# First expert layer in the order of falling tile counts, with weight splits in that order, early biases on TensorE and a double-buffered gate

## The chip, the cores and the metric

The kernel runs on one core of one Trainium2 chip. The metric is the device time in microseconds of one execution; times below are medians of several runs, and durations inside the kernel come from one profiled execution. The engines are TensorE (PE; its weight loads are listed as PEld), VectorE (DVE), ScalarE (ACT), GpSimd (POOL) and SyncE (SP), which only issues DMAs. A name with a q behind it (ACTq) is the engine's sequencer.

## The reference

A macaron block on 4 x 256 tokens of width 512: a mixture-of-experts layer, an attention layer and the same mixture-of-experts layer again, each behind a layer norm and with a residual.

```python
def ffn(x, W_gate, b_gate, W_e, b_e):          # W_e: 8 experts of 512 x 512
    logits = x @ W_gate + b_gate
    _, top_idx = jax.lax.top_k(logits, 2)
    y_all = jax.nn.relu(jnp.einsum('bsd,edh->bseh', x, W_e) + b_e)
    y = jnp.take_along_axis(y_all, top_idx[..., None], axis=2)
    return y.mean(axis=2)

x = x + 0.5 * ffn(layernorm(x), W_gate, b_gate, W_e, b_e)
x = x + attention(layernorm(x), Wqkv, bqkv, Wo, bo)   # one head of width 128, softmax over 256 keys
x = x + 0.5 * ffn(layernorm(x), W_gate, b_gate, W_e, b_e)
```

With the reference's inputs the first layer routes 248, 221, 241, 282, 295, 279, 237 and 245 (token, expert) pairs to experts 0 to 7, which is 2, 2, 2, 3, 3, 3, 2 and 2 tiles of 128 rows.

## The kernel before

The 2048 (token, expert) pairs of a mixture layer are sorted by expert and cut into tiles of 128 rows, at most NS = 23 of them; what an expert leaves empty stays empty, and tiles that no expert needs are run with no rows in them. There is no scheduler: each engine has its own program, written out by hand, and semaphores (`hi_made`, `lo_made`, `tp_copied`, `exp_done`, `ypre_made`, `yrow_made`, ...) order them against each other. An engine's instructions run in the order in which its program has them, so what stands behind a wait is late with it.

**Gate** (`gate`, `copy_gate`, `copy_logits`, `fold_logits`, `choose`). For each of four batches of two tiles TensorE transposes x, ScalarE copies the transposes to `xt_gate`, TensorE multiplies by the gate weights (less their mean, `centre_gate_weights`), ScalarE copies the result to `logit_t`, and TensorE folds four partial sums. VectorE makes the logits, the two best experts and their one-hot rows. ScalarE also writes the normalised rows (`normalise`), which SyncE stores to DRAM (`xn_dram`) for the gathers.

**Routing** (`count`, `split_rank`, `tile_starts`, `slots`, `token_list`, `tokens`, `tile_experts`). TensorE counts pairs ahead of each pair; VectorE makes from it each pair's rank, the tiles of each expert (`ntile`), the first tile of each (`excl`, a running sum) and each pair's tile and row; one-hot rows (`row_hot`) and marks go to TensorE, whose 16 small matmuls bring out the token of every row (L905). `tokens` turns that into indices (`tok`), and `tile_experts` writes the expert of every tile (`eid`). `warm_up` is matmuls of ones that keep TensorE's clock up.

**Experts** (`experts` on each engine). For tile t GpSimd gathers 128 rows of `xn_dram` (L541), TensorE transposes them (L917), ScalarE copies them, rounded, to `xt_hi` (`hi_rows`, L687) and VectorE writes what is left to `xt_lo` (`lo_rows`, L1408). The float32 product is the sum of three: hi rows by hi weights, hi rows by lo weights, lo rows by hi weights, four matmuls each (L943). VectorE adds the expert's bias from `be_bc`, a table of all biases on all partitions (`bias`, L1416), ScalarE applies relu (`relu`, L697), and GpSimd scatters the rows to `z_dram` (L549). In two cases, `t >= NY[f]`, TensorE adds the bias itself. The expert's number is read from `eid` to a register with `value_load` by TensorE and, ahead of `bias`, by VectorE.

The weights are loaded once, in 16 halves of an expert (`raw`, `load_half`), and split in the first layer: ScalarE rounds a half to `whi` (`split_hi`, L619), VectorE subtracts to `wlo` (`split_lo`, L379). Before, the halves are split in their own order: nine `hi` halves ahead of the first tile and one in each of the following, four `lo` halves ahead and two in each of tiles 0 to 5. Tile t may belong to expert t, so its product waits for the halves of experts 0 to t:

```python
if f == 0 and t < E:
    pe.wait_ge(hi_made, 2 * (t + 1))
    pe.wait_ge(lo_made, 2 * (t + 1))
```

In a tile ScalarE's program is `hi_rows(t + 1)`, `relu(t)`, split; VectorE's is `lo_rows(t + 1)`, `bias(t)`, splits.

**Second layer.** Its routing runs under the attention of the last batch. The first NA = 5 tiles are listed from the first three batches' pairs alone (`slots_early`, `token_list(1)`, `tokens(1)`), so that their gathers start before the last batch is through.

## Time and profile before

| | us |
|---|---|
| median of 3 runs | 277.38 (276.53 to 281.84) |
| the profiled execution | 278.46 |
| its span, first to last instruction | 276.6 |
| mean granted TensorE clock, share of full speed | 0.958 |
| busy: TensorE, VectorE, ScalarE, GpSimd | 243.6, 162.8, 108.2, 126.5 |

The profiled execution is 1.08 us above the median and 1.86 us longer than its span. Busy time is a sum over stages with different limits, so it doesn't say which engine a stage waits for; the chain of waits and the engines' timelines do.

### The profile page before, as it was taken

What the parts mean: (1) busy time and instruction counts of PE and PEld (TensorE: products, weight loads), DVE (VectorE), ACT (ScalarE), POOL (GpSimd) and SP (SyncE); (2) the same over time, 40 slices, a digit from 0 to 9 for tenths busy, and PEclk for the clock granted to TensorE, in tenths of its full rate; (3) what the DMA queues carried; (4) which work ended last, traced back from release to release, by engine and by line L of the source; (5) the groups of instructions that cost most, each with busy time, mean ns of one, the idle gap of its engine ahead of it and who ended that gap; (6) DMA issues with size and microseconds to landing.
All of it is one profiled execution on the core that took longest, in us unless ns stands there. A gap on an engine that the chain in (4) does not pass through costs nothing.

```text
span 276.6 us, 4889 instructions
## 1 busy us (share of the span) xinstructions
PE 243.6 (88%) x1319; PEld 181.5 (66%) x1320; DVE 162.8 (59%) x403; ACT 108.2 (39%) x192; POOL 126.5 (46%) x161
## 2 busy tenths in 40 slices
PE   6757979998999999989999995879989999999940
PEld 3543447677888888748778754347758888888730
DVE  2735679897444444766777766453963344444591
ACT  2756745454343333222336554105333433333310
POOL 5410174775665563324145510071377656664240
PEclk9995799999999999999999998699999999999995
DMA  5998889944784356154401022034246434547994
GB/s 144 396 368 309 307 253 378 359 139 150 246 262 131 124 158 186 61 154 152 152 4 46 31 78 76 0 100 150 95 152 200 164 126 135 164 126 208 334 355 172
DMA packets 22918, 49.40 MB, mean 179 GB/s; under 512 B 4460, under 2 KB 5100, under 8 KB 22640
## 3 DMA queue, kind: packets, MB, share of 16 engines
q1 hardware_dynamic: 13712, 26.55, 27.3%
q0 software_dynamic: 7360, 20.46, 23.3%
q10 hardware_dynamic: 1824, 2.12, 2.1%
q8 instruction: 11, 0.18, 0.3%
q14 instruction: 11, 0.09, 0.1%
HBM read 34.43 MB, written 18.35 MB: 191 GB/s over the span
## 4 chain that ended last, share of the span: by engine, by line
PE 67%; DVE 14%; ACT 5%; DMA 5%; issue 5%; DVEq 2%; POOL 1%; ACTq 1%; POOLq 0%
PE y_ps L943 18%; PE qk_ps L943 17%; PE tp_ps L917 6%; DVE wlo L379 5%; PE qk_ps L1018 5%; PE sp_ps L823 3%; PE tp_ps L844 3%; PE v_ps L1029 3%; DMA xg_late<-xn_dram,tok 2%; DMA bg_bc<-in_L_ffn_b_gate_dram 2%; PE y_ps L1068 2%; PE sp_ps L1056 2%; DVE ypre L1416 2%; PE g_ps L857 1%; PE sp_ps L1040 1%
## 5 line engine op out<-in xcount | busy, mean ns | idle before, releaser
L541 POOL DMA_INDIRECT xg<-xn_dram,tok x23 | 27.4, 1192 | 30.6 <-DVE tok L1330 17.9
L541 POOL DMA_INDIRECT xg_late<-xn_dram,tok x23 | 22.6, 984 | 29.5 <-DVE tok L1330 15.8
L549 POOL DMA_INDIRECT z_dram<-yrow,place x23 | 24.5, 1065 | 22.1 <-ACT yrow L697 14.4
L1408 DVE TENSOR_TENSOR xt_lo_late<-tp_ps,xt_hi_late 128x512 fp32r<-128x512 f32 x23 | 15.9, 691 | 27.9 <-ACT xt_hi_late L687 27.9
L697 ACT ACTIVATE yrow<-ypre 128x512 f32<-128x512 f32 x22 | 13.9, 633 | 44.0 <-DVE ypre L1416 44.0
L549 POOL DMA_INDIRECT z_dram<-xn,place x16 | 17.2, 1074 | 21.1 <-ACT xn L697 15.3
L1408 DVE TENSOR_TENSOR xt_lo<-tp_ps,xt_hi 128x512 fp32r<-128x512 f32 x23 | 15.9, 689 | 18.4 <-ACT xt_hi L687 18.4
L379 DVE TENSOR_TENSOR wlo<-raw,whi 128x1024 fp32r<-128x1024 f32 x16 | 18.8, 1218 | 2.6 <-POOL behind L569 2.1
L697 ACT ACTIVATE xn<-ypre_late 128x512 f32<-128x512 f32 x14 | 8.8, 632 | 26.9 <-DVE ypre_late L1416 25.8
L687 ACT ACTIVATE xt_hi_late<-tp_ps 128x512 fp32r<-128x512 f32 x23 | 13.4, 584 | 11.7 <-PE tp_ps L917 11.7
L1164 DVE BATCH_NORM_STATS2 stats<-x 128x6 f32<-128x512 f32 x24 | 15.6, 683 | 2.2 <-DMA x<-in_L_attn_x_dram 1.9
L619 ACT ACTIVATE whi<-raw 128x1024 fp32r<-128x1024 f32 x16 | 16.0, 1042 | 0.0
L1018 PE MATMUL qk_ps<-xt_att,wqkv 128*128 128x256 f32 x64 | 15.6, 390 | 0.4 <-ACT xt_att L671 0.4
L917 PE MATMUL tp_ps<-ident,xg_late 128*128 128x128 f32 x92 | 13.8, 274 | 2.2 <-DMA xg_late<-xn_dram,tok 2.2
L943 PE MATMUL y_ps<-whi,xt_hi 128*128 x48 | 14.5, 423 | 1.3 <-DVE wlo L379 1.3
L823 PE MATMUL sp_ps<-ones 128*128 128x512 bf16 x50 | 15.1, 462 | 0.0
L917 PEld LDWEIGHTS tp_ps<-ident,xg_late 128*128 128x128 f32 x92 | 11.1, 141 | 5.9 <-DMA xg_late<-xn_dram,tok 3.1
L917 PE MATMUL tp_ps<-ident,xg 128*128 128x128 f32 x92 | 13.9, 273 | 1.1 <-DMA xg<-xn_dram,tok 1.1
L943 PE MATMUL y_ps<-whi,xt_hi_late 128*128 x48 | 14.4, 421 | 0.5 <-ACT xt_hi_late L687 0.5
L687 ACT ACTIVATE xt_hi<-tp_ps 128x512 fp32r<-128x512 f32 x23 | 13.4, 582 | 3.5 <-PE tp_ps L917 3.5
L529 POOL TENSOR_TENSOR rstd<-var_eps,neg_half 128x2 f32<-128x2 f32 x12 | 8.9, 740 | 12.7 <-DVE var_eps L1179 12.1
L917 PEld LDWEIGHTS tp_ps<-ident,xg 128*128 128x128 f32 x92 | 11.3, 140 | 4.8 <-DMA xg<-xn_dram,tok 2.0
(197 smaller groups left out, 547.4 us busy)
## 6 DMA issues: line engine op xcount, KB each, us to landing
raw<-in_L_ffn_W_e_dram SPq DMA_DIRECT2D x16, 512.0 KB, 8.5
z_rows<-z_dram SPq DMA_DIRECT2D x6, 512.0 KB, 3.7
x<-in_L_attn_x_dram SPq DMA_DIRECT2D x8, 256.0 KB, 6.6
be_bc<-in_L_ffn_b_e_dram SPq DMA_DIRECT2D x2, 1024.0 KB, 9.5
xn_dram<-xn ACTq DMA_DIRECT2D x8, 256.0 KB, 2.0
whi<-z_dram SPq DMA_DIRECT2D x4, 512.0 KB, 5.3
wlo<-z_dram SPq DMA_DIRECT2D x4, 512.0 KB, 6.6
out_dram<-x SPq DMA_DIRECT2D x8, 256.0 KB, 3.0
```

The costliest lines, as they stand in the source:

```text
L379: eng.tensor_tensor(half(wlo, n), half(raw, n), half(whi, n).bitcast(F32), ALU.subtract).then_inc(done, 1)
L541: pool.indirect_dma_start(out=xg_at(f, t % XG), out_offset=None, in_=xn_dram[f][0:T - S if f and t < NA else T, :], in_offset=bass.Indirec ...
L549: pool.indirect_dma_start(out=z_dram[f][:, :], out_offset=bass.IndirectOffsetOnAxis(ap=place[:, t:t + 1], axis=0), in_=yrow_at(f, t % YB), ...
L619: act.activation(half(whi, n), half(raw, n), ACT.Copy).then_inc(hi_made, 1)
L687: act.activation(xt_hi_at(f, t % 2), tp_ps[(n0 + t) % 2][:], ACT.Copy).then_inc(tp_copied, 1)
L697: act.activation(yrow_at(f, t % YB), ypre_at(f, t % 2) if t < NY[f] else y_ps[t % 2][:], ACT.Relu, scale=HALF_MEAN).then_inc(yrow_made, 1)
L823: pe.matmul(bank[:], ones[:], ones[:].unsqueeze(1).broadcast_to([P, 4, P]), start=True, stop=True)
L917: last = pe.transpose(tp_ps[(n0 + t) % 2][:, c * P:(c + 1) * P], xg_at(f, t % XG)[:, c * P:(c + 1) * P], ident[:])
L943: last = pe.matmul(y_ps[t % 2][:], rows[:, c * P:(c + 1) * P], w[:, bass.ds(e * WE + c * H, H)], start=(n == 0), stop=(rows is lo and c == ...
L1018: last = pe.matmul(qk_ps[:, j * S:(j + 1) * S], wqkv[:, c, j * D:(j + 1) * D], xt_att[:, c, :], start=(c == 0), stop=(c == NC - 1))
L1164: read.append(step(dve.bn_stats(stats[:, s + i, :], x[:, TB * b + i, :])))
L1408: dve.tensor_tensor(xt_lo_at(f, t % 2), tp_ps[(n0 + t) % 2][:], xt_hi_at(f, t % 2).bitcast(F32), ALU.subtract).then_inc(xt_made, 1)
```

## The change

- **Order.** `tile_starts(0)` no longer takes a running sum over the experts. It makes a key of each expert from its tile count and its number, compares all pairs of keys (`bigger`), and sums the tile counts of the experts ahead (`excl`): experts come by falling count, ties by number. `order_experts` writes the expert at each place to `turn`, and twice that plus two, the number of halves that must have landed. `tile_experts_ordered` makes `eid` from both ends of each expert's stretch. `places` goes by `start_t`, so that the pairs' two halves of `z_dram` follow the new order; it moves from ahead of `tile_starts` to inside `slots`.
- **Splits.** `split_hi` and `split_lo` take the expert from `turn` by `value_load`. `split_hi` waits for one semaphore, `landed_halves`, which SyncE raises in the order of the halves. By the falling order the first 2E tiles need one new expert for two tiles; product t waits for `2 * (t // 2 + 1)` halves. Ahead of the first tile four `hi` and two `lo` halves are split; then `HI_IN_TILE` and `LO_IN_TILE`. VectorE's and ScalarE's heads of straight code are ten tiles (`HEADS`) and no longer eight.
- **Biases.** In tiles 0 to 3 of layer one TensorE adds the bias, from rows in three bf16 parts (`be_rows`, made by ScalarE and GpSimd) picked by `sel`; relu then reads the product itself. The tables `be_bc` are loaded after all halves, since their space serves the gate's second buffer, the gate weights' staging and `be_raw` until then.
- **Gate.** `xt_gate_at` and `gate_ps_at` alternate between two buffers and two banks in layer one, and the programs of TensorE and ScalarE are written out in a new order. Three tiles of x come by ScalarE's queue and the gate bias by SyncE's. The filling matmuls stand between the counts, 4, 5 and 6, and 18 ahead of the list, in place of 6 and 14.
- **Second layer.** ScalarE's copy for the gate goes ahead of a normalised tile and of two stores; the counts go ahead of projection matmuls; `slots_early` takes `score_max` into its middle; `token_list(1)` runs ahead of `mix_v`, ScalarE's mark ahead of `copy_prob`; filling matmuls, 3 and 7, stand around the scores. The third row buffer of the layer is a slot of `xn` (`yrow_at`).

```diff
+    BIAS_PE = (list(range(4)) + [NS - 1], [NS - 2, NS - 1])
+    BIAS_FROM = min(t for t in range(NS) if t not in BIAS_PE[0])
...
-        HI_AHEAD = 9
-        LO_AHEAD = 4
-        LO_IN_TILE = [2, 2, 2, 2, 2, 2]
+        HI_AHEAD = 4
+        LO_AHEAD = 2
+        HI_IN_TILE = [2, 2, 2, 2, 1, 1, 1, 1]
+        LO_IN_TILE = [2, 2, 2, 2, 1, 1, 1, 1, 1, 1]
+        X_BY_SP = 5
...
+            for i in range(X_BY_SP):
                 sp.dma_start(x[:, i, :], x_rows[i * P:(i + 1) * P, :]).then_inc(x_in_sem[i], 16)
+            sp.dma_start(bg_bc[:], b_gate.partition_broadcast(P)).then_inc(gate_bias_in, 16)
             for n in range(LOAD_FIRST):
                 load_half(n)
+            sp.wait_ge(be_zeroed, 1)
+            for first in (0, BE_LO, 2 * BE_LO):
+                sp.dma_start(be_raw[first:first + E, :], b_e).then_inc(be_rows_in, 16)
             for i in range(NT):
                 sp.wait_ge(xg_made, i + 1)
                 sp.dma_start(xn_dram[0][i * P:(i + 1) * P, :], xn_at(i)).then_inc(xn_stored[i], 16)
-            load_be(0)
+            def report_landed(first, end):
+                for n in range(first, end):
+                    sp.wait_ge(raw_in[n], 16)
+                    sp.sem_inc(landed_halves, 1)
             for n in range(LOAD_FIRST, LOAD_AHEAD):
                 load_half(n)
+            report_landed(0, LOAD_AHEAD)
...
+            sp.wait_ge(gate_done, B)
+            sp.wait_ge(be_rows_made, 2)
+            load_be(0)
             load_be(1)
+            report_landed(LOAD_AHEAD, 2 * E)
...
             def split_hi(n):
-                act.wait_ge(raw_in[n], 16)
-                act.activation(half(whi, n), half(raw, n), ACT.Copy).then_inc(hi_made, 1)
+                if n == 0:
+                    act.wait_ge(turn_made, 1)
+                e = act.value_load(turn[0:1, 0, n // 2:n // 2 + 1], min_val=0, max_val=E - 1)
+                if n % 2 == 0:
+                    loaded = act.value_load(turn[0:1, 1, n // 2:n // 2 + 1], min_val=2, max_val=2 * E)
+                    act.wait_ge(landed_halves, loaded)
+                act.activation(half_of(whi, e, n), half_of(raw, e, n), ACT.Copy).then_inc(hi_made, 1)
...
                 for t in range(head + first * STEP):
                     tile(t)
-                    if hi_left:
-                        split_hi(hi_left.pop(0))
+                    if f == 0 and t < len(HI_IN_TILE):
+                        for _ in range(HI_IN_TILE[t]):
+                            split_hi(hi_left.pop(0))
...
-                        pe.wait_ge(ypre_made, read)
-                    if f == 0 and t < E:
-                        pe.wait_ge(hi_made, 2 * (t + 1))
-                        pe.wait_ge(lo_made, 2 * (t + 1))
+                        pe.wait_ge(yrow_made if t - 2 in BIAS_PE[f] else ypre_made, read)
+                    if f == 0 and t < 2 * E:
+                        pe.wait_ge(hi_made, 2 * (t // 2 + 1))
                     n = 0
-                    if t >= NY[f]:
-                        pe.matmul(y_ps[t % 2][:], ident[:], be_bc[:, bass.ds(e * H, H)], start=True, stop=False)
+                    if t in BIAS_PE[f]:
+                        if f == 0 and t < BIAS_FROM:
+                            pe.matmul(y_ps[t % 2][:], sel[:, bass.ds(e, 1)].broadcast_to([BE_ROWS, P]),
+                                      be_rows[:], start=True, stop=False)
+                        else:
+                            pe.matmul(y_ps[t % 2][:], ident[:], be_bc[:, bass.ds(e * H, H)], start=True, stop=False)
...
+                        if w is wlo:
+                            if f == 0 and t < 2 * E:
+                                pe.wait_ge(lo_made, 2 * (t // 2 + 1))
...
+            copy_gate(0, 0)
+            copy_gate(0, 1)
+            copy_logits(0, 0)
+            normalise_batch(0, 0)
+            copy_gate(0, 2)
+            copy_logits(0, 1)
+            normalise_batch(0, 1)
+            copy_gate(0, 3)
+            copy_logits(0, 2)
+            copy_logits(0, 3)
+            normalise_batch(0, 2)
+            normalise_batch(0, 3)
+            bias_rows_high()
             mark_partition(0)
-            for n in his:
+            for n in range(HI_AHEAD):
...
+            count(0, 0)
+            warm_up(4, sp_ps)
+            count(0, 1)
+            warm_up(5, sp_ps)
+            count(0, 2)
             warm_up(6, sp_ps)
-            for b in range(B):
-                count(0, b)
-            warm_up(14, sp_ps)
+            count(0, 3)
+            warm_up(18, sp_ps)
             token_list(0)
...
+            count(1, b - 1)
+            warm_up(3, y0_ps)
             scores(b)
-            count(1, b - 1)
+            warm_up(7, y0_ps)
             transpose_prob(b)
+            token_list(1)
             mix_v(b)
-            project_out(b, lambda: token_list(1))
+            project_out(b)
...
+            def order_experts():
+                link(dve.tensor_reduce(position, bigger[0:1], AX_X, ALU.add))
+                link(dve.tensor_tensor(at_turn, position.unsqueeze(1).broadcast_to([1, E, E]),
+                                       iota_e[0:1, :].unsqueeze(2).broadcast_to([1, E, E]), ALU.is_equal))
+                link(dve.tensor_tensor(at_turn, at_turn, iota_e[0:1, :].unsqueeze(1).broadcast_to([1, E, E]),
+                                       ALU.mult))
+                link(dve.tensor_reduce(turn_f, at_turn, AX_X, ALU.add))
+                step(dve.tensor_copy(turn[:, 0, :], turn_f))
+                link(dve.tensor_scalar(turn[:, 1, :], turn_f, 2.0, 2.0, ALU.mult, ALU.add))
+                dve.engine_nop().then_inc(turn_made, 1)
...
+                    tile_step = step(dve.scalar_tensor_tensor(out=key[:], in0=ntile[:], scalar=float(E),
+                                                              in1=from_last[:], op0=ALU.mult, op1=ALU.add))
+                    dve.wait_ge(dve_step, rank_step)
+                    rank_row(B - n, n).then_inc(row_made, n)
+                    dve.wait_ge(dve_step, tile_step)
+                    tile_step = step(dve.tensor_tensor(bigger, key[:].unsqueeze(1).broadcast_to([P, E, E]),
+                                                       key[:].unsqueeze(2).broadcast_to([P, E, E]), ALU.is_gt))
+                    step(rank_tile(B - n, n))
+                    dve.wait_ge(dve_step, tile_step)
+                    link(dve.tensor_tensor(ahead_of, bigger, ntile[:].unsqueeze(1).broadcast_to([P, E, E]),
+                                           ALU.mult))
+                    link(dve.tensor_reduce(excl[:], ahead_of, AX_X, ALU.add))
...
+            def split_lo(n):
+                e = dve.value_load(turn[0:1, 0, n // 2:n // 2 + 1], min_val=0, max_val=E - 1)
+                dve.wait_ge(hi_made, n + 1)
+                dve.tensor_tensor(half_of(wlo, e, n), half_of(raw, e, n), half_of(whi, e, n).bitcast(F32),
+                                  ALU.subtract).then_inc(lo_made, 1)
...
-            places(0, B)
             tile_starts(0)
             slots(0)
+            order_experts()
             tokens(0)
-            tile_experts(0)
+            tile_experts_ordered()
             dve.wait_ge(first_issued, 1)
             for n in range(LO_AHEAD):
-                split_lo(dve, n, lo_made)
+                split_lo(n)
...
-            slots_early()
+            slots_early(lambda: score_max(b))
```

The new order of instructions at three places. First ScalarE, from its mark of the partitions to its second tile of layer one. Before:

```order
L677 ACTIVATE mark<-in_tile,part_id 128x368
L619 ACTIVATE whi<-raw 128x1024 x6
L687 ACTIVATE xt_hi<-tp_ps 128x512
L619 ACTIVATE whi<-raw 128x1024
L687 ACTIVATE xt_hi<-tp_ps 128x512
L697 ACTIVATE yrow<-ypre 128x512
L619 ACTIVATE whi<-raw 128x1024
L687 ACTIVATE xt_hi<-tp_ps 128x512
L697 ACTIVATE yrow<-ypre 128x512
L619 ACTIVATE whi<-raw 128x1024
```

After, from the first copy of rows on (the four splits that stand ahead of it read in the same way; L672 and L674 read the expert and the landed count, L676 is the split):

```order
L753 ACTIVATE xt_hi<-tp_ps 128x512 x2
L765 ACTIVATE yrow<-y_ps 128x512
L672 TENSOR_LOAD turn
L672 ISA x2
L674 TENSOR_LOAD turn
L674 ISA x2
L676 ISA
L676 ACTIVATE whi<-raw 128x1024
L672 TENSOR_LOAD turn
L672 ISA x2
L676 ISA
L676 ACTIVATE whi<-raw 128x1024
```

Every split has one or two register reads ahead of it, two splits stand in a tile where one stood, and the relu of tile 0 reads the product itself. Second, VectorE between the second set of one-hot rows and its first splits. Before:

```order
L1281 TENSOR_TENSOR row_hot<-iota_r,slot_r 128x1024
L1327 TENSOR_SCALAR place_lo<-g_ps 128x23
L1329 TENSOR_TENSOR place<-g_ps,place_lo 128x23
L1330 TENSOR_SCALAR tok<-place 128x23
L1289 TENSOR_TENSOR passed<-iota_t,incl 1x184
L1291 TENSOR_REDUCE eid_f<-passed 1x23
L1292 TENSOR_SCALAR eid<-eid_f 1x23
L379 TENSOR_TENSOR wlo<-raw,whi 128x1024 x4
```

After (`used` and `picked` serve `order_experts` as scratch):

```order
L1378 TENSOR_TENSOR row_hot<-iota_r,slot_r 128x1024
L1386 TENSOR_REDUCE used<-above 1x8
L1387 TENSOR_TENSOR picked<-used,iota_e 1x64
L1389 TENSOR_TENSOR picked<-picked,iota_e 1x64
L1391 TENSOR_REDUCE used<-picked 1x8
L1392 CAST turn<-used 1x8
L1393 TENSOR_SCALAR turn<-used 1x8
L1394 ISA
L1452 TENSOR_SCALAR place_lo<-g_ps 128x23
L1454 TENSOR_TENSOR place<-g_ps,place_lo 128x23
L1455 TENSOR_SCALAR tok<-place 128x23
```

The order of the experts (L1386 to L1393) stands ahead of the token arithmetic. Third, TensorE from the last projection of attention to the second layer's first transposes. Before:

```order
L1018 MATMUL qk_ps<-xt_att,wqkv 128x256 x2
L1040 MATMUL sp_ps<-qk 128x256 x2
...
L1048 MATMUL sp_ps<-ident,prob 128x128 x4
L1056 MATMUL sp_ps<-pt,v 128x256 x2
L1068 MATMUL y_ps<-wo,prob 128x512
L905 MATMUL v_ps<-mark_a,row_hot 128x10 x12
L1068 MATMUL qk_ps<-wo,prob 128x512
L823 MATMUL sp_ps<-ones 128x512 x11
L917 MATMUL tp_ps<-ident,xg_late 128x128 x4
```

After:

```order
L1100 MATMUL qk_ps<-xt_att,wqkv 128x256 x2
...
L893 MATMUL y_ps<-ones 128x512 x3
L1122 MATMUL sp_ps<-qk 128x256 x2
L893 MATMUL y_ps<-ones 128x512 x7
L1130 MATMUL sp_ps<-ident,prob 128x128 x4
L974 MATMUL v_ps<-mark_a,row_hot 128x10 x12
L1138 MATMUL sp_ps<-pt,v 128x256 x2
L1150 MATMUL y_ps<-wo,prob 128x512
L1150 MATMUL qk_ps<-wo,prob 128x512
L893 MATMUL sp_ps<-ones 128x512 x11
L986 MATMUL tp_ps<-ident,xg_late 128x128 x4
```

The list (`v_ps<-mark_a,row_hot`) moved from between the output matmuls to behind the transposes of `prob`, and ten filling matmuls are new.

## Rows read from the trace of the kernel before

**Rows 1.** The page: engines' busy time; a costly group (count | busy us, mean ns | idle).
```profile
PE 243.6 (88%) x1319; PEld 181.5 (66%) x1320; DVE 162.8 (59%) x403; ACT 108.2 (39%) x192; POOL 126.5 (46%) x161
...
L379 DVE TENSOR_TENSOR wlo<-raw,whi 128x1024 fp32r<-128x1024 f32 x16 | 18.8, 1218 | 2.6 <-POOL behind L569 2.1
```

**Rows 2.** Chain of waits in order of time: start us, us, what.
```profile
7.37 1.07 PE v_ps L864 x8
...
25.82 5.81 PE sp_ps L823 x14
...
179.92 3.47 DMA xg_late<-xn_dram,tok
```

**Rows 3.** Timelines of ScalarE and TensorE, end of the gate: start us, us, instruction.
```profile
16.82 1.09 ACT L654 ACTIVATE xt_gate<-tp_ps 128x512 f32<-128x512 f32 x2 [1.98 <-PE tp_ps L844]
...
19.83 2.92 ACT L632 ACTIVATE xn_more<-x,off,rstd 128x512 f32<-128x512 f32 x4
...
19.98 0.61 PE L871 MATMUL g_ps<-fold,logit_t 128*128 128x8 f32 x4 [0.50 <-ACT logit_t L663]
```

**Rows 4.** Timeline of VectorE, routing of layer one.
```profile
23.27 0.22 DVE L1248 TENSOR_TENSOR picked<-onehot,rk_ps 128x64 f32<-128x64 bf16 x1 [3.18 <-PE rk_ps L894]
...
25.30 1.22 DVE L1281 TENSOR_TENSOR row_hot<-iota_r,slot_r 128x1024 bf16<-128x1024 bf16 x1
...
26.81 0.21 DVE L1248 TENSOR_TENSOR picked<-onehot,rk_ps 128x64 f32<-128x64 bf16 x1
...
29.88 1.22 DVE L1281 TENSOR_TENSOR row_hot<-iota_r,slot_r 128x1024 bf16<-128x1024 bf16 x1
```

**Rows 5.** Timeline of TensorE: token list, first product, products of tiles 9 and 10.
```profile
31.46 0.57 PE L905 MATMUL g_ps<-mark,row_hot 128*128 128x46 bf16 x16
...
38.19 1.19 PE L943 MATMUL y_ps<-whi,xt_hi 128*128 x4 [0.32 <-DVE wlo L379]
...
71.95 1.17 PE L943 MATMUL qk_ps<-whi,xt_hi 128*128 x4
...
75.18 1.17 PE L943 MATMUL y_ps<-whi,xt_hi 128*128 x4
```

**Rows 6.** Timeline of GpSimd: the first gather.
```profile
32.98 1.22 POOL L541 DMA_INDIRECT xg<-xn_dram,tok  x1 [17.85 <-DVE tok L1330]
```

**Rows 7.** Timelines of VectorE and ScalarE around tile 4.
```profile
57.17 0.69 DVE L1408 TENSOR_TENSOR xt_lo<-tp_ps,xt_hi 128x512 fp32r<-128x512 f32 x1
...
58.02 0.69 DVE L1416 TENSOR_TENSOR ypre<-y_ps,be_bc 128x512 f32<-128x512 f32 x1 [0.15 <-issue]
...
58.74 0.63 ACT L697 ACTIVATE yrow<-ypre 128x512 f32<-128x512 f32 x1 [1.67 <-DVE ypre L1416]
59.28 1.04 ACT L619 ACTIVATE whi<-raw 128x1024 fp32r<-128x1024 f32 x1
60.23 0.58 ACT L687 ACTIVATE xt_hi<-tp_ps 128x512 fp32r<-128x512 f32 x1
```

**Rows 8.** VectorE's sequencer in the bias (L1412), all of it: ns min/median/max.
```profile
L1412 DVEq TENSOR_LOAD <-eid x43: 299/306/1142, 41.5 to 257.1; - x43
```

**Rows 9.** Stretches: length, busy PE, PEld, DVE, ACT, POOL, clock share, DMA, GB/s.
```profile
21.10:24.50 3.40, 2.43 (x28) 1.40 (x26) 1.06 (x8) 3.40 (x5) 0.00 (x0) 0.50 0.80 294
...
171.30:174.70 3.40, 2.17 (x7) 1.59 (x8) 3.16 (x19) 1.09 (x4) 0.00 (x0) 0.50 0.00 0
```

**Rows 10.** Timeline of VectorE and TensorE ahead of the second layer.
```profile
169.84 0.69 DVE L1523 TENSOR_REDUCE soft<-sp_ps 128x2 f32<-128x512 f32 x1 [1.60 <-PE sp_ps L1040]
...
173.64 2.07 PE L1056 MATMUL sp_ps<-pt,v 128*128 128x256 f32 x4 [0.69 <-ACT pt L756]
...
174.54 0.68 DVE L1281 TENSOR_TENSOR row_hot<-iota_r,slot_r 128x512 bf16<-128x512 bf16 x1
...
178.05 0.47 PE L905 MATMUL v_ps<-mark_a,row_hot 128*128 128x10 bf16 x12
...
184.92 1.21 PE L943 MATMUL y_ps<-whi,xt_hi_late 128*128 x4 [0.19 <-ACT xt_hi_late L687]
```

269 lines of the change are left out of this document (179 added, 90 removed).

## The prediction

> **What bounds the kernel now.** I read the page first: TensorE is busy for 88% of the span [rows 1], so I asked where it runs at its own pace and where it waits. The chain of waits answers in order of time. From tile 8 of the first expert layer on, TensorE is never late: one tile's matmuls follow the last one's after 3.23 us (71.95, 75.18) [rows 5]. There less work would help, and the change takes none away. Three stretches are not TensorE's. (a) **Before the first product**, at 38.19 us: the gate, which starts late because the gate weights' sum waits for the gate bias (7.37 us) and then goes back and forth between TensorE and ScalarE, 3.34 us a batch; then routing on VectorE, with 14 filling matmuls of TensorE as the last step ahead of the token list at 31.46 [rows 2, 5]. (b) **Tiles 0 to 8 of layer one**: tile 0 starts at 38.19 us and tile 9 at 71.95 us, 33.8 us for nine tiles that TensorE could do in nine times 3.23, 29.0. Two things set it, each 3.7 us long: VectorE's two splits of 1.22 us with bias and low rows of 0.69 each [rows 1, 7]; and a cycle from VectorE's bias (58.02) over ScalarE's relu (58.74), its half of a weight (59.28) and its copy of rows (60.23) to the next low rows and bias [rows 7]. (c) **Ahead of the second layer**: TensorE waits for scores, softmax and the first gather, and its clock is at half after 171 us [rows 9, 10].
>
> **Routing, the gate.** Two buffers and two banks let a batch's transposes run under the last one's gate. ScalarE becomes the limit: two copies (1.0 from start to start), logits 0.3, two normalised tiles 1.4 [rows 3], 2.7 us a batch. From about 9.6 us (a second batch of x that can't be used earlier) twice 2.7, then 1.3, then gate, copy and fold of the last batch, 1.6: the last fold ends at about 17.9, where it ended at 20.59 [rows 3].
>
> **Routing, VectorE.** Count, four filling matmuls and count end near 19.4. Then ranks and choose (2.0 from 23.27 to 25.30) and one-hot rows (1.2) [rows 4] bring the second rank pick to 22.7; before, it was 26.81. From there to the last one-hot rows before took 26.81 to 31.10, 4.3 us. Added on that path: comparing 64 keys, a product and a reduction of 64 in place of two steps of 8 (0.6 us by their neighbours of 0.2), and the places, moved here behind the slots (0.4). 22.7 + 5.3 makes 28.1 for 31.10. Next stands the ordering of the experts, seven linked steps, 1.5 us, ahead of the token arithmetic: TensorE's list (0.57) is hidden under it. Tokens end at 30.3, before at 32.68; GpSimd's gather starts 0.3 later and its rows are there 3.5 us after its start, at about 34.1 [rows 5, 6].
>
> **Routing, what is late next.** The table of tile experts grows to three steps over 368 elements, some 2.8 us against 0.9, and ends at 33.1, before the rows land: hidden. ScalarE is late next. Its first split now waits for the order, at 29.6, and it does four in a row ahead of the first copy of rows. Each reads the expert's number into a register. ScalarE never does so in this trace. The nearest row is VectorE's read: a TENSOR_LOAD of 306 ns in the median, once 1142 [rows 8], and register work behind it: the bias starts 0.85 us after the low rows ahead of it (57.17, 58.02), which keep the engine for 0.69 [rows 7]. The lower bound is nothing (it runs ahead under an activation of 1.04 us), the upper is that 1.14. I take 0.55, since an engine that has just passed its semaphore starts the read only then: before the bias, the read starts with the operation ahead of it. An even half reads twice (number and landed count): 1.3 us. So the splits start at 31.0, 32.0, 33.3 and 34.2, the copy at 35.2, and the first product at 35.9 for 38.19: **2.3 us earlier**. Loading x by two queues, and the bias rows that GpSimd and ScalarE make (some 5 us of GpSimd's, idle from 15 to 33), I cost at nothing: they lie beside that work, and if they ended after 30 us the gather would wait for them.
>
> **Tiles 0 to 8.** The order of falling counts asks two halves for two tiles, not for one. The reference's counts make it 3, 4, 5, 0, 1, 2, 6, 7, so the third expert's halves are numbers 10 and 11, whose loads start after the first gather, as before. They are needed on ScalarE near 40.8; with their issue 2.4 us earlier they should be there by 40.4. VectorE gets lighter: two splits and the low rows, 3.1 us, with no bias in tiles 0 to 3. TensorE pays one more matmul of 0.23 us for four tiles. ScalarE gets heavier: relu, two reads (1.3), split, read (hidden), split, copy of rows. From the end of product t to the start of product t + 2 it needs 3.9 us, which TensorE's 3.5 a tile doesn't cover: about 3.7 us a tile, as before. From tile 4 on the bias is on VectorE again and the cycle closes: copy 0.6, bias 0.8 after it and 0.7 long, relu, read of 1.3 or 0.7, split. By the durations of [rows 7] the starts of products follow each other by 4.4, 3.8, 4.4 and 3.8 us, where before they took 3.7. Added up, tile 9 starts 34.9 us after tile 0, against 33.8: **1.1 us lost**, although half as many splits are asked. If the reads hid wholly, 9 times 3.23 and 4 times 0.23 would be 30.0. Both bias tables load now after the halves; by their rate they are there at about 54.5, when VectorE comes for them; up to 1.5 us late is in the range.
>
> **Ahead of the second layer.** Three moves. The gate copy no longer stands behind ScalarE's issue of two stores, and the count goes ahead of two projection matmuls: scores are there 0.7 us earlier than at 169.84. The slots' first steps run while VectorE would wait for scores, 1.6 us of idle [rows 10]. The list of tokens runs ahead of the mixing of V, when the last one-hot rows are made: these end at 172.7 for 175.22. The list before ran at 178.05, between the output matmuls. Tokens then end at 173.8, and the first gather goes out at 174.6 for 179.92 and lands at 178.1 for 183.4 [rows 2, 10]. What is late next: the output projection and its residual, which the table of experts stands behind. Ten more filling matmuls cover the waits, and I take the clock to stay at full. Then four transposes end at 171.7, the list at 173.2, V's mix takes 1.0 for 2.07, the projection likewise half of before and ends at 176.3, the table is there at 179.1, warm-up ends at 178.7, and transposes and copy bring the first product to 180.1 for 184.92: **4.9 us earlier**. All behind it hangs on that product.
>
> **Sum.** 2.3 - 1.1 + 4.9 = 6.1 us. The profiled execution took 278.46 us (span 276.6 and 1.9 around it), 1.1 above the median; 272.4 for it is 271.3 on the median of 277.38.
>
> **Rivals.** *The reads hide.* If ScalarE's sequencer reads while it waits, stretch (b) takes 30.0 us: 4.9 less, 266.4. Against it speaks where VectorE's reads stand in the trace: none starts before the wait ahead of it ends.
> *The filling stays at half clock.* The clock was at half from 21.1 us and still in the 14 filling matmuls, 0.42 us each [rows 2, 9], after a gate in which TensorE stood between its matmuls. The change makes the gate denser and puts 33 filling matmuls in for 20. If the clock falls all the same, 18 of them at 0.43 us hold the list to 33.6 where it stood at 31.46, and the first gain turns from 2.3 to a loss of 2.1: 275.7.
> *The second transition keeps its half clock.* Transposes, mix (2.07) [rows 10] and projection stay as long as they were; the earlier list alone leaves the first product at 182.2: 273.5.
> *Slower than before: dear reads.* The cost is ScalarE's, from turn_made to tile 7. With loads of twice the median, four that count ahead of the first copy add 1.5 us, three in each of tiles 0 to 3 add 3.6, and six in tiles 4 to 7 add 1.8: 6.9 us, 278.2. It passes the time before from a load of 0.57 us on. For it speaks VectorE's longest load, 1.14 [rows 8]; against it their median.
> The Trainium skill (DMA: Bandwidth & Descriptors, Latency and other measured facts) gives a tensor_load a floor of some 600 ns. By that rule this rival is the forecast; the trace's median of 306 ns disagrees.
>
> **How the numbers follow.** Forecast 271.3, chance 0.45, its own range 269.3 to 273.3 (0.7 each way for x's arrival, 1.5 for late bias tables). Hidden reads 0.13; half clock in the first filling 0.14; in the second 0.14; dear reads 0.07; the rest, 0.07, is mixtures. The range 267.5 to 276 takes the forecast, both clock cases and part of the first, some 0.8. A change of 2%, to 271.8, is about what a measurement of this kernel can tell from none. Faster by over 2%: 0.28 of the forecast's 0.45, hidden reads at 0.13 and 0.05 of mixtures, 0.46. Slower by over 2%, above 282.9, needs loads over 0.8 us: 0.03. Within 2%: 0.51.
>
> **What the profile would show.** Last fold at about 18; full clock from 14 to 30 us; first product near 36; TENSOR_LOAD rows on ScalarE near 0.3 us and idle time of some 0.7 us ahead of the first split of a tile; tile 9 starting near 70.8; full clock from 168 to 180 and the gain growing by 4 to 5 us up to the first late product. I am wrong if tiles 4 to 7 run at 3.2 us, if the clock row shows 0.5 in either filling, or if splits wait for landed_halves or VectorE for the bias tables.

## The result

The changed kernel takes **282.3 us** (281.55 to 285.81, 4 runs) where the kernel before takes 276.97 (276.53 to 281.84, 4 runs): ratio 1.0183, 95% interval 1.0145 to 1.0221. It is slower, by 5.3 us; whether by more than 2% the interval leaves open. The forecast was 271.3, its range 267.5 to 276.0. The profiled execution took 281.96 us, span 279.7, mean granted clock 0.964; a second trace of the same program, taken later, 283.52 and 281.3. Disturbed runs are left out of the comparisons.

The page of the changed kernel has the same engine times as before, within 5 us [rows 1], so the loss has to be looked for stage by stage, in waits and in work at half clock.

```profile
PE 247.4 (88%) x1346; PEld 184.0 (66%) x1347; DVE 165.7 (59%) x413; ACT 109.1 (39%) x194; POOL 130.7 (47%) x173
```

TensorE's timeline (... stands for rows left out), which answers to [rows 5] and the last row of [rows 10] (list, first product, tiles 1, 2, 5 to 10, first late product):

```profile
30.93 0.37 PE L974 MATMUL g_ps<-mark,row_hot 128*128 128x46 bf16 x8 [0.70 <-DVE row_hot L1378]
...
39.21 2.06 PE L1018 MATMUL y_ps<-whi,xt_hi 128*128 x4
...
43.53 1.25 PE L1018 MATMUL qk_ps<-whi,xt_hi 128*128 x4
...
49.17 0.39 PE L1001 MATMUL y_ps<-be_rows,sel 72*128 72x512 bf16 x1 [2.09 <-ACT xt_hi L753]
...
60.32 0.97 PE L1018 MATMUL qk_ps<-whi,xt_hi 128*128 x3 [0.17 <-ACT xt_hi L753]
...
64.76 1.19 PE L1018 MATMUL y_ps<-whi,xt_hi 128*128 x4 [0.94 <-ACT xt_hi L753]
...
68.66 1.19 PE L1018 MATMUL qk_ps<-whi,xt_hi 128*128 x4 [0.41 <-ACT xt_hi L753]
...
72.98 1.19 PE L1018 MATMUL y_ps<-whi,xt_hi 128*128 x4 [0.83 <-ACT xt_hi L753]
...
76.88 1.20 PE L1018 MATMUL qk_ps<-whi,xt_hi 128*128 x4 [0.40 <-ACT xt_hi L753]
...
80.13 1.17 PE L1018 MATMUL y_ps<-whi,xt_hi 128*128 x4
...
185.04 1.22 PE L1018 MATMUL y_ps<-whi,xt_hi_late 128*128 x4 [0.24 <-ACT xt_hi_late L753]
```

The first product comes at 39.21 for 38.19, tile 10 at 80.13 for 75.18, the first late product at 185.04 for 184.92. So 1.0 us is lost up to the first product, 3.9 from there to tile 10, and 4.8 is gained in the second transition. Two more losses stand behind it: 0.6 in the second layer, and 2.4 at the end, where GpSimd's last scatter took 3.81 us. 1.0 + 3.9 - 4.8 + 0.6 + 2.4 is the 3.1 between the two spans (279.7, 276.6). The rest of the 5.3 between the medians: the profiled execution before lies 1.5 us above its median, the changed one 0.3 below, and the changed kernel takes 0.4 us more outside its span.

VectorE in the routing, which answers to [rows 4] (ranks, cast, rows; the same again; order of the experts; tokens), and GpSimd beside it:

```profile
20.79 0.22 DVE L1345 TENSOR_TENSOR picked<-onehot,rk_ps 128x64 f32<-128x64 bf16 x1 [2.77 <-PE rk_ps L963]
...
21.30 0.72 DVE L1355 CAST rank_u<-rank_f 128x8 uint32<-128x8 f32 x1
22.12 0.57 DVE L1359 TENSOR_SCALAR slot_r<-rank_u 128x8 uint32<-128x8 uint32 x1
...
23.54 1.06 DVE L1321 TENSOR_TENSOR onehot<-iota_e,topi 128x32 bf16<-128x32 f32 x1
...
25.66 0.21 DVE L1345 TENSOR_TENSOR picked<-onehot,rk_ps 128x64 f32<-128x64 bf16 x1
...
29.66 1.22 DVE L1378 TENSOR_TENSOR row_hot<-iota_r,slot_r 128x1024 bf16<-128x1024 bf16 x1
...
31.84 0.15 DVE L1393 TENSOR_SCALAR turn<-used 1x8 int32<-1x8 f32 x1
...
32.46 0.18 DVE L1455 TENSOR_SCALAR tok<-place 128x23 uint32<-128x23 uint32 x1
...
20.84 1.15 POOL L635 TENSOR_TENSOR be_bc<-be_bc,be_rows 72x512 f32<-72x512 f32 x1 [6.50 <-ACT be_rows L683]
22.06 0.60 POOL L636 CAST be_rows<-be_bc 32x512 bf16<-32x512 f32 x1
...
23.40 1.15 POOL L638 TENSOR_TENSOR be_rows<-be_bc,be_rows 8x512 bf16<-8x512 f32 x1
...
33.52 1.22 POOL L568 DMA_INDIRECT xg<-xn_dram,tok  x1 [8.97 <-DVE tok L1455]
```

Three of VectorE's small steps (21.30, 22.12 and 23.54) take 0.4 to 0.9 us more than the same steps before, which took 0.17, 0.17 and 0.19, and each ends when a step of GpSimd on the bias rows ends: 22.02 beside 21.99, 22.69 beside 22.66, 24.60 beside 24.55.

Two waits between 39 and 50 us (engine, line, what for: us, times, longest), the splits that the first of them held, and TensorE's clock in two stretches (length, busy times, clock share, DMA share, GB/s):

```profile
ACT whi L676 <- SPq L435: 2.4, 1, 2.4
PE y_ps L1001 <- ACT xt_hi L753: 2.1, 1, 2.1
```

```profile
46.55 2.00 ACT L676 ACTIVATE whi<-raw  x2 [2.36 <-SPq L435]
```

```profile
16.00:24.00 8.00, 7.47 (x53) 3.96 (x46) 4.03 (x23) 3.81 (x7) 2.95 (x4) 0.57 1.05 381
...
36.00:42.00 6.00, 4.81 (x16) 3.29 (x17) 2.99 (x3) 2.02 (x3) 1.98 (x3) 0.72 0.73 191
```

L435 is the report of landed halves. After the relu of tile 0 ScalarE reads its registers until 44.64 us and then stands until 46.44 for halves 10 and 11, which the third expert in line needs; its copy of rows for tile 2 stands behind these splits. With GpSimd's hold on VectorE and these halves, the half clock is the third loss: the first product's four matmuls take 2.06 us for 1.19 in [rows 5].

From tile 0 to tile 10, of the 3.9 us lost 0.6 is in tile 0 (half clock), 1.9 in tile 1 (the wait for the halves) and 1.4 in tiles 2 to 9, where ScalarE's register reads are (reads_ahead, below).

### The profile page after: what moved, and what is told of

It is laid out like the page before. It is cut to its first block, busy times and chain, and to the rows that moved or that the text cites. A ratio compares the mean times of both kernels' runs of the same rounds, so it can differ in the third digit from the quotient of the medians.

```text
span 279.7 us, 5124 instructions
## 1 busy us (share of the span) xinstructions
PE 247.4 (88%) x1346; PEld 184.0 (66%) x1347; DVE 165.7 (59%) x413; ACT 109.1 (39%) x194; POOL 130.7 (47%) x173
## 4 chain that ended last, share of the span: by engine, by line
PE 64%; DVE 9%; DMA 7%; ACT 6%; issue 6%; POOLq 1%; ACTq 1%; POOL 1%; SPq 1%; DVEq 1%
PE y_ps L1018 17%; PE qk_ps L1018 17%; PE tp_ps L986 5%; PE qk_ps L1100 5%; DMA raw<-in_L_ffn_W_e_dram 5%; PE tp_ps L914 3%; PE v_ps L1111 3%; PE rk_ps L893 2%; PE y_ps L1150 2%; PE sp_ps L893 1%; POOLq L51 1%; PE sp_ps L1138 1%; DMA xg<-xn_dram,tok 1%; DMA xg_late<-xn_dram,tok 1%; DVE row_hot L1378 1%
## 5 line engine op out<-in xcount | busy, mean ns | idle before, releaser
L576 POOL DMA_INDIRECT z_dram<-xn,place x23 | 26.6, 1158 | 26.9 <-ACT xn L765 17.8
L576 POOL DMA_INDIRECT z_dram<-yrow,place x23 | 25.3, 1101 | 25.3 <-ACT yrow L765 19.5
L568 POOL DMA_INDIRECT xg<-xn_dram,tok x23 | 23.6, 1028 | 25.9 <-PE tp_ps L986 12.8
L765 ACT ACTIVATE xn<-ypre_late 128x512 f32<-128x512 f32 x21 | 13.3, 632 | 41.6 <-DVE ypre_late L1564 41.2
L765 ACT ACTIVATE yrow<-ypre 128x512 f32<-128x512 f32 x18 | 11.4, 632 | 35.2 <-DVE ypre L1564 35.2
L1547 DVE TENSOR_TENSOR wlo<-raw,whi x16 | 19.2, 1224 | 4.9 <-ACT whi L676 2.3
L676 ACT ACTIVATE whi<-raw x16 | 16.2, 1052 | 8.5 <-issue 5.5
L893 PE MATMUL sp_ps<-ones 128*128 128x512 bf16 x63 | 17.1, 423 | 0.0
L1018 PE MATMUL y_ps<-whi,xt_hi 128*128 x48 | 15.4, 444 | 1.8 <-ACT xt_hi L753 1.8
L556 POOL TENSOR_TENSOR rstd<-var_eps,neg_half 128x2 f32<-128x2 f32 x12 | 8.9, 740 | 12.8 <-DVE var_eps L1275 12.1
```

Of the source, the lines that this page charges most:

```text
L568: pool.indirect_dma_start(out=xg_at(f, t % XG), out_offset=None, in_=xn_dram[f][0:T - S if f and t < NA else T, :], in_offset=bass.Indirec ...
L576: pool.indirect_dma_start(out=z_dram[f][:, :], out_offset=bass.IndirectOffsetOnAxis(ap=place[:, t:t + 1], axis=0), in_=yrow_at(f, t % YB), ...
L676: act.activation(half_of(whi, e, n), half_of(raw, e, n), ACT.Copy).then_inc(hi_made, 1)
L765: act.activation(yrow_at(f, t % YB), y_ps[t % 2][:] if t in BIAS_PE[f] else ypre_at(f, t % 2), ACT.Relu, scale=HALF_MEAN).then_inc(yrow_ma ...
L893: pe.matmul(bank[:], ones[:], ones[:].unsqueeze(1).broadcast_to([P, 4, P]), start=True, stop=True)
L1018: last = pe.matmul(y_ps[t % 2][:], rows[:, c * P:(c + 1) * P], w[:, bass.ds(e * WE + c * H, H)], start=(n == 0), stop=(rows is lo and c == ...
```

## The experiments

Thirteen kernels ran, two of them with a second trace. The table has each trace's stages in us: VectorE's first pick of ranks, tokens ready, start of tiles 0, 1, 2 and 10, first late product, TensorE's last end, length of the last scatter, span; and the median of its runs. A ratio behind a time is to the kernel before, run beside it: its medians were 277.7, 277.7 and 277.4, and 280.6 beside third_gather.

| kernel | ranks | tokens | tile 0 | tile 1 | tile 2 | tile 10 | late | PE end | scatter | span | median |
|---|---|---|---|---|---|---|---|---|---|---|---|
| before | 23.3 | 32.7 | 38.2 | 41.9 | 45.7 | 75.2 | 184.9 | 266.0 | 1.40 | 276.6 | 277.0 |
| before_again | 25.5 | 34.4 | 39.9 | 43.6 | 47.5 | 76.9 | 185.7 | 267.6 | 2.60 | 279.5 | one run |
| changed | 20.8 | 32.6 | 39.2 | 43.5 | 49.3 | 80.1 | 185.0 | 266.7 | 3.81 | 279.7 | 282.3 |
| after_again | 21.7 | 33.8 | 39.9 | 43.4 | 50.9 | 84.4 | 189.3 | 270.7 | 1.41 | 281.3 | 282.4 |
| low_early | 18.7 | 29.2 | 35.3 | 38.8 | 46.1 | 78.4 | 183.3 | 264.9 | 1.40 | 275.6 | 278.3 |
| halves_early | 18.6 | 30.7 | 36.8 | 40.3 | 44.3 | 76.3 | 181.2 | 262.6 | 1.40 | 273.5 | 277.0 |
| reads_ahead | 21.6 | 33.7 | 39.7 | 43.3 | 50.4 | 81.0 | 186.0 | 267.5 | 1.41 | 278.1 | 279.7 |
| scatter_gap | 20.8 | 32.6 | 39.1 | 43.5 | 49.1 | 80.0 | 185.0 | 266.5 | 0.98 | 276.8 | 280.1 |
| gate_filled | 19.5 | 31.6 | 37.6 | 41.1 | 48.4 | 79.3 | 184.2 | 265.7 | 1.40 | 277.2 | 280.8 |
| third_gather | 21.7 | 33.7 | 39.9 | 43.3 | 52.4 | 83.7 | 188.7 | 270.0 | 1.40 | 280.7 | 281.8 |
| four | 21.7 | 32.2 | 38.2 | 41.7 | 45.7 | 75.1 | 180.0 | 261.7 | 0.98 | 272.0 | 274.7 |
| four_fill | 22.1 | 32.3 | 38.4 | 42.0 | 45.9 | 75.2 | 180.1 | 261.3 | 0.98 | 271.6 | 273.7 |
| late_only | 23.6 | 32.5 | 38.0 | 41.7 | 45.6 | 75.2 | 180.0 | 262.6 | 1.40 | 273.2 | 275.7 |
| gate_late | 18.8 | 27.9 | 34.8 | 38.9 | 43.2 | 72.5 | 177.3 | 261.4 | 1.40 | 272.1 | 273.3 |
| gate_late_fill | 21.7 | 30.7 | 36.9 | 40.2 | 44.4 | 73.9 | 178.8 | 260.2 | 0.98 | 270.5 | 270.5 |

The column of first ranks moves by 3.1 us between programs whose gate is the same (18.6 in halves_early, 21.7 in after_again), and by 2.2 between two traces of the kernel before. So stages are compared from row to row of one trace, not by their absolute times.

### low_early: GpSimd's bias rows out of VectorE's way

```diff
-            for n in range(LOAD_FIRST):
+            for n in range(3):
...
             copy_logits(0, 2)
+            bias_rows_high()
             copy_logits(0, 3)
             normalise_batch(0, 2)
             normalise_batch(0, 3)
-            bias_rows_high()
```

> The changed kernel, with the bias rows of layer one made earlier: ScalarE rounds them ahead of its copy of the fourth batch's logits, so that GpSimd's four steps on them end before VectorE picks the first ranks. Theory (shared port): in the changed kernel VectorE's cast (0.72 us for 0.17), its next step (0.57 for 0.17) and its one-hot step (1.06 for 0.19) each ended when a GpSimd step on the bias rows ended; 1.8 us of the routing is this. They go back to 0.17 to 0.19 here, the second pick of ranks comes at 23.9 for 25.66, the first product at 37.4 for 39.21, and the time falls by 1.8 us to 280.5. Rival (not the port): the long steps belong to this point of VectorE's program or to the half clock around it; they stay long, GpSimd or not, and the time stays at 282.3.

Measured 278.28 us, 1.0048 of the kernel before (0.9999 to 1.0097). VectorE in it:

```profile
19.21 0.42 DVE L1357 CAST rank_u<-rank_f 128x8 uint32<-128x8 f32 x1
19.73 0.17 DVE L1361 TENSOR_SCALAR slot_r<-rank_u 128x8 uint32<-128x8 uint32 x1
...
20.97 0.19 DVE L1323 TENSOR_TENSOR onehot<-iota_e,topi 128x32 bf16<-128x32 f32 x1
...
18.44 1.15 POOL L640 TENSOR_TENSOR be_rows<-be_bc,be_rows 8x512 bf16<-8x512 f32 x1
```

The long steps are gone, but for one, and that ends with GpSimd's last (19.63 beside 19.59). From the first ranks to the tokens it takes 10.5 us; in the seven traces that have the bias rows late, 11.8 to 12.1. So GpSimd's steps beside VectorE's cost 1.3 to 1.6 us, shown, whichever of VectorE's steps is hit. The gain of 4.0 us over the changed kernel, where 1.8 was expected, is not all this edit's: the first ranks themselves are 2.1 us earlier, as they are in halves_early without it. And of the first product's 3.9 us only 1.8 is left at tile 10, because tile 2 waits for the halves all the longer (46.1 - 38.8 = 7.3 us for tile 1).

### halves_early: the late halves

```diff
-        LOAD_AHEAD = 10
-        LOAD_BETWEEN = 12
+        LOAD_AHEAD = 12
+        LOAD_BETWEEN = 14
```

> The changed kernel, with halves 10 and 11 loaded straight behind halves 6 to 9 and not behind the first gather (12 and 13 behind the first, 14 and 15 behind the second). Theory: tile 0's split waits for landed_halves from 44.64 to 46.44 us because these two halves are asked for only after the first gather has landed; without it the third product starts 1.8 us earlier and the time falls to 280.5. Rival (the next one is late too): the four halves behind them or the gather, which then shares the queues with more weights, take the wait's place; the gain is under 0.5 us, 281.8 or more.

Measured 276.97 us, 0.997 of the kernel before (0.9917 to 1.0023): level with it. Tile 1 takes 4.0 us, where it takes 5.7 to 7.5 in the six traces with the loads as the change has them. The rival fell: ScalarE's wait for the report is 0.5 us. From tile 0 to tile 10 it takes 39.5 us, the changed kernel 40.9 and 44.5 in its two traces, the kernel before 37.0; so the wait is shown, and the reads' share stays. More than the expected 1.8 came back: 5.3 us between the medians. The wait is longer in the second trace of the changed kernel (below), and this trace has early first ranks and a short last scatter; how the 5.3 divides is not shown.

### reads_ahead: the register reads

```diff
                     if t + 1 < NS:
                         hi_rows(t + 1, n0 + t + 2, f * NS + t or None)
+                    if f == 0 and t < len(HI_IN_TILE):
+                        for n in hi_left[:HI_IN_TILE[t]]:
+                            turn_read.append(read_turn(n))
...
                     relu(t, ypre_no(f, t) + 1, sent(t) or None)
```

> The changed kernel, with ScalarE's register reads for a tile's splits put ahead of the relu of that tile and not behind it. Theory (reads on the cycle): tiles 4 to 7 follow each other by 4.44, 3.90, 4.32 and 3.90 us because a split comes 0.55 or 1.3 us after the relu; with the reads done under the wait for the product they fall to the 3.7 us that VectorE's bias and ScalarE's copy set before, 1.8 us less, 280.5. Rival (reads are hidden anyway, VectorE's splits set the pace): the starts of the products stay as far apart as they are, 282.3.

Measured 279.69 us, 1.0077 (1.0039 to 1.0114). Four successive tiles:

```profile
63.35 1.17 PE L1029 MATMUL qk_ps<-whi,xt_hi 128*128 x4
...
66.84 1.25 PE L1029 MATMUL y_ps<-whi,xt_hi 128*128 x4
...
70.49 1.19 PE L1029 MATMUL qk_ps<-whi,xt_hi 128*128 x4
...
74.14 1.19 PE L1029 MATMUL y_ps<-whi,xt_hi 128*128 x4 [0.16 <-ACT xt_hi L760]
...
77.79 1.19 PE L1029 MATMUL qk_ps<-whi,xt_hi 128*128 x4 [0.16 <-ACT xt_hi L760]
```

Tiles 5 to 9 follow each other by 3.49, 3.65, 3.65 and 3.65 us, for 4.44, 3.90, 4.32 and 3.90: 2.1 us, where the theory had 1.8. The reads were on the cycle, and placed under the wait for the product they cost nothing that shows here.

### scatter_gap: the last scatter

```diff
             for i in range(NT):
+                if i == 3:
+                    dve.wait_ge(last_issued, 1)
                 dve.wait_ge(lower_added, i // 2 + 1)
```

> The changed kernel, with VectorE waiting, ahead of the fourth of its last eight additions, until GpSimd has issued the last scatter. Theory (VectorE's additions hold the scatter): the last scatter took GpSimd 3.81 us, from 268.10 to 0.86 us after VectorE's last addition, where the kernel before had gaps between the additions and took 1.40; with the gap it takes about 1.4, the end of GpSimd's program, 7.6 us after it, comes 2.3 us earlier, and the time falls to 280.0. Rival (the scatter is slow by itself, by its rows or its queue): it still takes 3.8 us, VectorE only loses the wait, and the time is 282.3 to 283.

Measured 280.12 us, 1.0110 (1.0055 to 1.0166). GpSimd's last scatter in the changed kernel and VectorE's additions beside it:

```profile
268.10 3.81 POOL L576 DMA_INDIRECT z_dram<-xn,place  x1 [2.15 <-ACT xn L765]
...
266.15 2.49 DVE L1735 TENSOR_TENSOR x<-x,whi 128x512 f32<-128x512 f32 x4
268.56 2.49 DVE L1735 TENSOR_TENSOR x<-x,wlo 128x512 f32<-128x512 f32 x4
```

With the pause:

```profile
267.89 0.98 POOL L578 DMA_INDIRECT z_dram<-xn,place  x1 [2.16 <-ACT xn L769]
...
268.98 0.69 DVE L1741 TENSOR_TENSOR x<-x,whi 128x512 f32<-128x512 f32 x1 [1.17 <-POOL behind_last L616]
```

The scatter takes 0.98 in all four kernels that have the pause. Without it, it takes 1.40 in nine of eleven traces, 2.60 in one and 3.81 in one, and the additions stand at the same places beside it in most of them: each of these scatters ends 0.86 us behind the end of an addition. For 3.81 it is the last of the eight (271.05), for 2.60 the sixth, for 1.40 the fourth, the first that ends after the scatter began. So VectorE's additions do hold the scatter, and which of their ends lets it in is chance, different from one execution to the next. It is a loss of 2.4 us in the profiled run, not one of the change. That the median fell by 2.2 us as well, as expected, is not explained by it: the second trace of the changed kernel has 1.41, where the pause could save 0.4.

### gate_filled: the clock in the gate

```diff
             transpose_xn("g0", 2, 1, 2)
+            warm_up(2)
             transpose_xn("g0", 3, 0, 1)
             gate(0, 2)
             fold_logits(0, 1)
+            warm_up(2)
             transpose_xn("g0", 3, 1, 2)
+            warm_up(3)
             gate(0, 3)
+            warm_up(2)
```

> The changed kernel with nine more filling matmuls (2, 2, 3 and 2) in TensorE's gaps between the transposes of the third and fourth batch and the gates, where it waits 0.5 to 0.8 us for ScalarE. Theory (the clock falls because TensorE stands in the gate): the granted clock stays full from 14 to 24 us, the first ranks are picked near 19.0 for 20.79, and the mean clock of a run rises from 0.965 to 0.98; 280.5. Rival (where the clock falls doesn't hang on these gaps but on where a run stands when it starts): clock and time are as they were, or 0.5 us longer for the matmuls, 282.3 to 282.8.

Measured 280.79 us, 1.0153 (1.0104 to 1.0202), clocks 0.971 to 0.978 for 0.961 to 0.969. The gate ran at full clock here, but it did so too in after_again without these matmuls. In both traces the clock fell behind a gap of 2.3 us ahead of the list instead (26.4 to 28.8 us here, half from 29.5 to 32.9). So it is inconclusive on the gate.

### four and four_fill: the mends together

four has the four edits above except the fillings. four_fill adds those, 24 filling matmuls ahead of the list for 18 and 26 behind it for 16.

> The changed kernel with the four edits tried so far together: bias rows early, halves 10 and 11 early, reads ahead of the relu, and VectorE's pause for the last scatter. Theory: they touch four different stretches, so the gains add: 1.3 (port) + 1.8 (landed halves) + 1.8 (reads) + 2.3 (last scatter) = 7.2, 275.1. Rival (the stretches depend on each other: an earlier first product meets the next late transfer, and the clock falls elsewhere): half of it, 278.5.

> The changed kernel with the four edits, the nine filling matmuls in the gate, 24 ahead of the list for 18 and 26 behind it for 16. Theory (the clock falls where TensorE stands, at the gate's end, ahead of the list and ahead of the first gather's landing): full clock from the gate to tile 9 in every run, mean clock 0.985 or more, and the time of the best run of the four edits (271.1) becomes the median. Rival (the clock's fall hangs on where an execution starts, not on these gaps; more fillings only hold the list up): 274.7 as before, or up to 1 us more.

four: 274.67 us, 0.9862 (0.9735 to 0.9989); 7.6 us under the changed kernel, 7.2 expected. Its runs lie from 271.12 to 275.35. That the two agree is luck: measured one by one, the edits' medians lay 4.0, 5.3, 2.6 and 2.2 us under the changed kernel's, 14.1 together, and half of that came of all four. So the gains don't add, as the rival said. four_fill: 273.67 us, 0.9846 (0.9789 to 0.9902), clocks 0.985 or 0.986 in every run. Its clock in the stretches where the changed kernel had 0.57 and 0.72:

```profile
16.00:24.00 8.00, 7.37 (x69) 4.36 (x69) 3.79 (x31) 5.81 (x11) 3.50 (x4) 1.00 0.89 329
...
36.00:42.00 6.00, 5.67 (x29) 3.50 (x27) 3.27 (x4) 2.30 (x4) 2.84 (x3) 1.00 0.71 194
```

Full clock in this trace and a mean of 0.985 in every run, as expected; the median did not reach the 271.1 of four's best run, and the 1.0 us to four's median is within the noise of either.

### late_only, gate_late, gate_late_fill: the parts without the order

The kernel before with the second layer's hunks of the change; with those of the first gate as well; and with more fillings and the pause, by which the third differs from the second:

```diff
-        WARM = [16, 0, 0]
+        WARM = [26, 0, 0]
...
-            warm_up(18, sp_ps)
+            warm_up(24, sp_ps)
```

> The kernel before with the second layer's parts of the change alone: the gate copy ahead of the stores, the counts ahead of projection matmuls, 3 and 7 filling matmuls around the scores, the maximum of the scores inside the early slots, the mark and the token list ahead of the mixing of V. Expert order, splits, biases and the first gate are as before. Theory: this part is worth what the prediction gave it, 4.9 us from the last product of layer one to the first late product (69.6 us before, 64.6 in the changed kernel), and nothing of it is given back: 272.5 on a median of 277.4. Rival (it shows only behind the changed layer one, or its half clock comes back without it): under 2.5 us, 275 or more.

> The kernel before with the second layer's parts and the first gate of the change: two buffers and two banks, x by two queues, the gate bias by the other queue, 4, 5, 6 and 18 filling matmuls. Expert order, splits and biases are as before. Theory: without the ordering (about 1.1 us between the first and the second rows) and without GpSimd's bias rows (1.3 to 1.8 us), the gate's gain comes through: first ranks at 20.8 at the latest for 23.27, first product near 35.5 for 38.19, 270 in all. Rival (the weights are late next: nine high and four low halves ahead of the first product, which have to land first): the first product stays near 38 and the time is that of the second layer's parts alone, 272.5.

> The kernel before with the second layer's parts and the first gate of the change, 24 filling matmuls ahead of the list for 18, 26 behind it for 16, and VectorE's pause for the last scatter. In the trace without these the clock was at half from 32.5 to 37 us, after TensorE had stood 2.24 us ahead of the first gather's rows; the first product's four matmuls took 1.98 us for 1.19. Theory: the clock stays full there, the first tile is 1.2 us shorter, and the last scatter, at 1.40, gets 0.4 shorter: 271.8 for 273.3. Rival: the fillings hold the list or the transposes up by as much, 273.3 to 274.3.

late_only: 275.7 us over ten scattered runs, 0.9904 (0.9851 to 0.9958), 272.5 expected. From tile 10 to the first late product it takes 104.8 us for 109.7, the whole 4.9, but the rows of the second layer's tile 5 then took 5.4 us from issue to landing (3.3 in the kernel before) and 1.5 us was lost again behind it. gate_late: 273.34 us, 0.987 (0.9815 to 0.9924), 270 expected: the first product at 34.8, though its four matmuls ran at half clock, 1.98 us; 3.0 us were lost again from the second layer's tile 5 on, whose rows took 5.5 us to land and behind which the clock was at half for 3.4 us. gate_late_fill: **270.54 us, 0.9743 (0.9694 to 0.9792)**, 271.8 expected, the best of all; its clock row is at 9 throughout, and TensorE has no gap ahead of the gather's rows. Its profiled execution, 272.2 us, is the slowest of its four:

```profile
PEclk9999999999999999999999999999999999999995
```

```profile
29.90 5.77 PE L846 MATMUL sp_ps<-ones 128*128 128x512 bf16 x26
35.51 0.60 PE L940 MATMUL tp_ps<-ident,xg 128*128 128x128 f32 x4
...
36.88 1.20 PE L966 MATMUL y_ps<-whi,xt_hi 128*128 x4
```

### after_again and before_again: what one trace is worth

> The changed kernel once more, unedited, for a second trace. Theory (its four losses are the program's own): clock at half in the gate's end and again at the first product, first ranks picked at 20.8, second at 25.7, 1.8 us of waiting for landed_halves in tile 0, the last scatter at 3.8 us; 282.3. Rival (part of them is the hazard of one execution): the port and the landed halves show again, but the clock falls elsewhere or the last scatter takes 1.4 us, and the time is nearer 280.

> The kernel before once more, unedited, for a second trace. Theory: the same stages within 0.5 us, the clock at half somewhere between 20 and 32 us, first product at 38.2, first late product 184.9 less what the first stage gains, 276.5 to 278. Rival: where the clock falls moves a stage by over 1 us.

after_again: 282.39 us, 1.0155 (1.0089 to 1.0222). The losses by GpSimd's bias rows (12.1 us from ranks to tokens) and of the halves are there again, the latter far larger: tile 1 takes 7.5 us, ScalarE waits 3.6 us for the report where it waited 1.8, and the clock is at half from 49 to 56 us behind it. The chain of waits shows whose wait it is:

```profile
34.70 3.59 DMA xg<-xn_dram,tok
...
38.73 9.29 DMA raw<-in_L_ffn_W_e_dram
```

The gate kept its full clock and the last scatter took 1.41, so those two were chance in the profiled run. The rival was right in this, but the time did not come nearer to 280. before_again, one run, took 281.22 us where 276.5 to 278 was expected; its first ranks are 2.2 us later than in the first trace, and 1.5 of this is there at 12 us, long before its clock fell. So a stage did move by over 1 us, as the rival said, but mostly not by the clock.

### third_gather: why the halves take so long

The first load asked for behind the first gather's landing takes 3.6 to 4.6 us to land in the five traces with splits in their own order, and 6.9 to 7.5 in the nine with ordered splits. In the five, VectorE's splits hold the third gather's issue (1.84 to 1.87 us; 0.95 in the nine). In four of them it so ends about 1.1 us behind the start of the load's issue (37.63 and 36.54 us in the kernel before). gate_late is the exception: there the gather's issue ended at 32.80, just ahead of the load's at 32.89, and the load still landed in 3.6 us. First the kernel before, then gate_late:

```profile
35.76 1.87 POOL L541 DMA_INDIRECT xg<-xn_dram,tok  x1 [0.21 <-issue]
```

```profile
30.96 1.84 POOL L552 DMA_INDIRECT xg<-xn_dram,tok  x1 [0.24 <-issue]
```

```diff
             for n in range(LOAD_AHEAD, LOAD_BETWEEN):
                 load_half(n)
+            sp.sem_inc(halves_asked, 1)
...
+                    if f == 0 and t == 2:
+                        pool.wait_ge(halves_asked, 1)
                     gather(f, t)
```

> The changed kernel, with GpSimd issuing the third gather only once SyncE has issued the loads of halves 10 and 11. In the seven traces of kernels with ordered splits the first load behind the first gather's landing took 6.9 to 7.5 us from issue to landing, in the five with splits in their own order 3.6 to 4.6; in those five VectorE's splits held the third gather's issue (1.85 us for 0.94), so that it ended behind the load's issue. Theory (the third gather's rows are fetched ahead of the weights when it is issued first, and cost them 3 us): with the gather behind, halves 10 and 11 land in 3.6 to 5 and 5 to 6.5 us, near 41.5 and 43.3 where the first product is at 39.2, the wait for landed_halves goes, and the time falls by 2 to 4 us to 278.3 to 280.3. Rival (the load's time is set by something else in the ordered kernels): 7 us again, the wait stays, and the time is 282.3 or, by the later third gather, a little more.

From issue to landing, least, median and most, of the six loads behind the first gather; first the kernel before (issued from 36.5 us), then the changed kernel (from 37.2), then this one (from 38.3). The least is the first load:

```profile
DMA to landing us min/median/max: 4.6/8.4/10.5
```

```profile
DMA to landing us min/median/max: 7.1/10.1/13.2
```

```profile
DMA to landing us min/median/max: 4.9/7.8/12.1
```

The first load lands in 4.9 us and ScalarE's wait for the report falls to 0.7, so in this kernel the gather ahead did cost the load 2 to 3 us, by one trace against nine. By gate_late, the order of the two issues is not all that sets it. And the third gather, now behind the loads, itself took 10.1 us, and tile 2 started later still (52.4). The median is 281.82 us, 1.0142 (1.0007 to 1.0276) of a kernel before whose runs beside it ranged from 275.7 to 282.3: no gain. Changing the order of the two moved the wait from the halves to the gather; what took it away in these runs was asking for the halves earlier.

## Why the prediction was wrong, point by point

The forecast was 6.1 us faster, and the profiled execution's span is 3.1 longer. Of these 9.2 us, 3.3 lie ahead of the first product (35.9 forecast, 39.2 measured) and 2.8 from there to tile 9 (34.9 forecast, 37.7 measured); 0.1 is the second transition, 0.6 lies in the second layer behind it and 2.4 in the last scatter, of which the sum had nothing.

**The second transition** was right, term and mechanism: 4.8 us for 4.9, full clock, first gather out at 179.30 in a layer that ran 5 us late; late_only shows it alone, though its median is only 2 us under the kernel before's.

**The reads and the cycle** were right. A split's read begins when the wait ahead of it ends (TENSOR_LOAD some 277 ns, the longest 500), and tiles 5 to 8 took 4.44, 3.90, 4.32 and 3.90 where the text had 4.4, 3.8, 4.4, 3.8, one tile sooner. That ScalarE takes the reads behind the relu was worth 2.1 us, which the sum had inside its 1.1. VectorE did not wait for the bias tables.

**The step that failed first** was "with their issue 2.4 us earlier they should be there by 40.4". The halves 10 and 11 landed at 44.3 and 46.4 us, and in the second trace at 45.8 and 48.0. Their issue was 0.6 us later than before, not earlier, since the gather was (33.52 for 32.98), and they took 7.1 and 8.8 us to land for 4.6 and 5.8. I had read the time to landing in the trace of the kernel before as a property of the load. third_gather shows that in this kernel it hangs on the gather ahead of it, which VectorE's splits no longer held; why gate_late's load was fast all the same stays open. The wait, 1.8 us in the profiled run and 3.6 in the second, where half clock follows it, is the loss whose mending gained most: halves_early takes it away and is level with the kernel before.

**The second failure** was "I cost at nothing: they lie beside that work". GpSimd's steps on the bias rows, 20.84 to 24.55 us, fell on VectorE's ranks and held three of its steps, 1.3 to 1.6 us: the second pick of ranks came 4.9 us behind the first, where the forecast had 3.3. I looked at GpSimd's idle time and not at what it shares. The Trainium skill (SBUF — State Buffer, Who interferes with whom) has VectorE and GpSimd share a pair of ports under an exclusive lock. By it a VectorE cast or tensor_scalar can take the pair, an operation with two inputs in SBUF contends with a GpSimd instruction that reads SBUF, and a reduction never contends. The trace agrees: the cast, the tensor_scalar and the one-hot step held here are of these kinds (0.72 us for 0.17, 0.57 for 0.17, 1.06 for 0.19), and the reduction and the maxima beside GpSimd's steps kept their length (0.22 and 0.16). The page spoke against the change, and I did not weigh it.

**The filling stays at half clock** was a rival at 0.14, and in the profiled run the clock did fall: 0.57 of full clock from 16 to 24 us, the first four fillings in 1.89 us, and again at the first product. In other traces the fall came elsewhere. What the rival priced did not happen: the eighteen fillings ahead of the list ran at full clock, in 4.04 us, and the list was not late by them. The first ranks came 1.4 us late (20.8 for 19.4), of which the fall explains 1.3 (last folds 1.02 us for 0.61, first fillings 1.89 for 1.02 in halves_early); ahead of the first product it cost some 1.0 more (transposes 0.88 us for 0.60, three fillings 1.49 for 0.81). With the 1.6 of the second failure, less 0.6 that the steps from the second ranks to the tokens were shorter than forecast, this is the 3.3 us of the first product: the tokens were ready at 32.6 for 30.3, and the first split could start only at 33.52 for 31.0. Without the order the first product is at 34.8 (gate_late) and 36.9 (gate_late_fill), with first ranks at 18.8 and 21.7.

**Slower by dear reads** was the rival on the right side, for a wrong reason: the loads were cheaper than its price.

**The order of the experts** bought nothing that these runs show. It halves the splits that are asked for per tile, but from tile 0 to tile 10 four_fill needs 36.8 us and gate_late_fill 37.0; ahead of it the order costs 1.2 us from ranks to tokens (10.3 for 9.0). The ordered kernel, mended, takes 273.7 in the median and the one without the order 270.5. They differ in the biases and the gate's nine fillings too, and their traces by 1.1 us of span only, so the 3.1 us is not shown to be the order's alone.

**Not settled:** what decides at which gap of an execution the clock falls. Of the twelve traces with the new gate it fell behind a gap of 2.2 to 2.4 us ahead of the first gather's rows in three (half from 37.5 us in the changed kernel), behind one of 2.3 us ahead of the list in five, and in or behind the wait ahead of tile 2 in four. In the profiled run and scatter_gap it fell in the gate as well. Behind gaps of 2.4 us ahead of those rows in the kernels four and low_early it did not fall, nor behind a wait of 3.7 us ahead of tile 2 in gate_filled, nor in the two kernels where fillings closed the gaps.

## What to carry to other kernels

A change that reorders work moves the moment at which each transfer is asked for and what is queued ahead of it: follow every DMA that a new order needs earlier, with its issue, its neighbours and its landing, before counting instructions. An engine that is idle is not free if it shares a port with one on the path. And two traces of an unedited kernel tell which of its waits are its own.

## What the hardware did that I had not expected

- A VectorE operation with two inputs in SBUF (`wlo<-raw,whi`, 1.22 us, or the additions at the end, 0.69) holds a gather or scatter that GpSimd begins while it runs: in these traces 120 issues beside such an operation took over 1.15 us, and each ended 0.82 to 0.90 us behind the end of one. Begun just behind a split's start it takes 1.8 to 2.0 us for 0.95, begun near the split's end it is hardly longer (0.94 at 38.34 us in the changed kernel), and a split that begins after it leaves it alone.
- TensorE's first matmuls run at half pace for a time that differs from run to run, while the granted clock reads 1.00: the same eight transposes in 1.17 us (halves_early) and 1.91 (reads_ahead), the same eight matmuls of the weights' sum in 0.96 and 1.72. The first ranks follow by up to 3 us.

```profile
4.92 1.17 PE L914 MATMUL tp_ps<-ident,x 128*128 128x128 f32 x8
5.92 0.96 PE L933 MATMUL v_ps<-be_bc 128*128 128x8 f32 x8
```

```profile
4.92 1.91 PE L925 MATMUL tp_ps<-ident,x 128*128 128x128 f32 x8
6.63 1.72 PE L944 MATMUL v_ps<-be_bc 128*128 128x8 f32 x8
```
